# Output projection and shared expert: transposes inside the group before, products two blocks ahead across the turn, first inputs fetched during attention

## The reference

```python
xn  = layernorm(x)
x   = x + attention(xn) @ W_o          # 16 heads of 16, causal
        + routed(xn)                   # 16 experts of inner width 1024, each takes its 512 best tokens
        + gelu(xn @ Sg.T) * (xn @ Su.T) @ Sd.T    # shared expert, inner width 512
```

## Time and profile before

| | us |
|---|---|
| median of three runs | 2456.82 |
| the profiled execution, its own time | 2440.34 |
| its span | 2438.2 |
| TensorE matmul busy | 2319.6 (95%) |
| VectorE busy | 1935.7 (79%) |
| ScalarE busy | 1502.7 (62%) |
| GpSimd busy | 241.9 (10%) |
| mean granted clock of TensorE | 0.967 |

### The profile page before, as it was taken

How to read it: one execution, slowest core, us unless ns; L and a number is a source line. 1 busy time by engine, 2 the same in 40 slices (tenths; PEclk the granted TensorE clock), 3 DMA queues, 4 the chain that set the end, 5 groups by cost and what they waited for, 6 DMA issues and landing times. The chain is left out here.

```text
span 2438.2 us, 53041 instructions
## 1 busy us (share of the span) xinstructions
PE 2319.6 (95%) x20269; PEld 1506.5 (62%) x20275; DVE 1935.7 (79%) x3721; ACT 1502.7 (62%) x2908; POOL 241.9 (10%) x228
## 2 busy tenths in 40 slices
PE   7987999999999999999999999987898999999997
PEld 4554555555555555555555555547787888888886
DVE  6775999999999898999999999946744666666664
ACT  2233677788877777888788887762233545454543
POOL 3000000000000000000001000001121223322332
PEclk9956999999999999999999999998899999999998
DMA  7854000003000005000001000002252444344534
GB/s 263 314 156 82 17 10 10 4 11 79 12 8 11 14 17 108 22 13 10 11 2 40 4 4 4 4 24 73 69 165 88 128 132 134 91 131 131 138 98 119
DMA packets 141910, 167.91 MB, mean 69 GB/s; under 512 B 53612, under 2 KB 107372, under 8 KB 141628
## 3 DMA queue, kind: packets, MB, share of 16 engines
q1 hardware_dynamic: 127916, 142.87, 19.2%
q0 software_dynamic: 13728, 22.28, 4.9%
q10 hardware_dynamic: 64, 0.02, 0.0%
HBM read 117.86 MB, written 48.56 MB: 68 GB/s over the span
## 5 line engine op out<-in xcount | busy, mean ns | idle before, releaser
L945 DVE TENSOR_REDUCE a_mp<-a_pm 128x1 f32<-128x512 f32 (+3 forms) x2176 | 1293.2, 663 | 81.5 <-PE a_pm L1112 55.7
L1070 ACT ACTIVATE a_p<-a_ps 128x512 f32<-128x512 f32 (+2 forms) x2176 | 1120.9, 587 | 372.6 <-PE a_ps L1193 265.8
L1112 PE MATMUL a_pm<-a_k,a_q 48*128 48x512 f32 (+3 forms) x2304 | 820.6, 447 | 7.8 <-ACT p_xs L379 1.2
L1193 PE MATMUL a_ps<-a_q,a_k 50*128 50x512 f32 (+3 forms) x2304 | 762.2, 428 | 24.4 <-DMA a_q<-a_nb 23.4
L1193 PEld LDWEIGHTS a_ps<-a_q,a_k 50*128 50x128 f32 x2304 | 378.4, 188 | 387.8 <-ACT a_p L1070 306.8
L1215 PE MATMUL a_po<-a_p,a_v 128*32 128x384 f32 (+2 forms) x8688 | 615.5, 386 | 0.9
L1112 PEld LDWEIGHTS a_pm<-a_k,a_q 48*128 48x128 f32 x2304 | 384.2, 190 | 53.7 <-DVE a_mp L945 39.4
L1215 PEld LDWEIGHTS a_po<-a_p,a_v 128*32 128x32 f32 x8688 | 202.7, 109 | 202.2 <-issue 134.4
L1590 ACT ACTIVATE e_g<-e_pg 128x512 f32<-128x512 f32 x128 | 76.6, 599 | 242.4 <-PE e_pu L1668 242.0
L1635 DVE TENSOR_TENSOR e_hf<-e_g,e_pu 128x512 f32<-128x512 f32 x128 | 88.0, 688 | 172.1 <-ACT e_g L1590 163.2
L1678 PE MATMUL e_po<-e_wdp,e_hp 128*128 128x256 f32 x1536 | 203.3, 284 | 0.0
(11 more groups left out here) (161 smaller groups left out, 1672.4 us busy)
## 6 DMA issues: line engine op xcount, KB each, us to landing
e_wgu<-in_wg SPq DMA_DIRECT2D x18, 1024.0 KB, 5.6
e_wgu<-in_wu SPq DMA_DIRECT2D x18, 1024.0 KB, 7.7
e_wd<-in_wd SPq DMA_DIRECT2D x18, 1024.0 KB, 10.0
a_q<-q_parts SPq DMA_DIRECT2D x180, 64.0 KB, 2.3
q_parts<-p_parts SPq DMA_DIRECT2D x16, 512.0 KB, 6.0
k_parts<-p_parts SPq DMA_DIRECT2D x16, 512.0 KB, 7.5
a_k<-k_parts SPq DMA_DIRECT2D x60, 128.0 KB, 3.6
v_padded<-p_v SPq DMA_DIRECT2D x8, 544.0 KB, 7.7
```

What stands on the lines that cost most here:

```text
L945: eng.tensor_reduce(mp[:, i, heads[0]:heads[-1] + 1, r, kc], ps[:, 0:len(heads) * w].rearrange("p (a n) -> p a n", n=w), AX.X, ALU.max).th ...
L1070: eng.activation(pr[:, i, heads[0]:heads[-1] + 1, off:GT], pS[n % HEADS][:, 0:len(heads) * w].rearrange("p (a n) -> p a n", n=w), ACT.Exp) ...
L1112: last = eng.matmul(ps[:, n * w:(n + 1) * w], QT[t % SLOTS][tile, a, r * P:(r + 1) * P], KT[g % 2][tile, a, kc * GT:kc * GT + w], start=n ...
L1193: last = eng.matmul(ps[:, m * w:(m + 1) * w], KT[TILES[t][0] % 2][tile, a, b * P:(b + 1) * P], QT[t % SLOTS][tile, a, off:GT], start=m == ...
```

## The change

1. The groups of tokens are taken in reverse: group g of the program is now the tokens of group 7 - g.
2. Three inputs are fetched during attention, behind the end of tile 27 of 0 to 31: tokens and attention rows of the first group and attention rows of the second. They lie in room that the queries (`a_qr`) and keys (`a_k`) of finished tiles have left. GpSimd makes the halves of the first group's tokens there too, at the end of its attention program.
3. TensorE's order in a group is projection, up 2, down 0, *turn 0 of the next group*, up 3, down 1, *turn 1 of the next*, *up 0 of the next*, down 2, down 3, *up 1 of the next*. `m_at` has two buffers. The very first second half is turned into `m_po`.
4. VectorE's order: block 1, block 2, low half 0 of the next group, block 3, low half 1 of the next, block 0 of the next, additions. ScalarE follows the same order.
5. GpSimd converts the tokens of group g once the four products of group g - 2 are through, instead of once its down products are. Each kind of input has a semaphore and a place in SP's queue of its own.
6. The loops over groups are written out.

The core of the diff (lines of before have -, of the changed kernel +):

```diff
+                    if w == OVER[LAST - 4] + 5:
+                        eng.wait_ge(s_pv, START[LAST - 3])
+                        for n in range(2):
+                            eng.wait_ge(s_as[n], 16 * 13)
+                        eng.dma_start(k.XT0.rearrange("p d n -> p (d n)"), k.xt[NG - 1]).then_inc(k.s_xt0, 16)
+                        for n, room in enumerate((k.A0, k.A1)):
+                            eng.dma_start(room, k.attn.rearrange("(g k p) d -> g p k d", k=TG, p=P)[NG - 1 - n]
+                                          ).then_inc(k.s_a0, 16)
...
+                eng.wait_ge(k.s_xt0, 16)
+                eng.tensor_copy(k.XP0[:, :, HIGH, :], k.XT0).then_inc(k.s_xp0, 1)
+                eng.wait_ge(k.s_xp0, 1)
+                low(eng, (k.XP0[:, :, HIGH, :], k.XP0[:, :, LOW, :]), k.XT0).then_inc(k.s_xp0, 1)
...
+        def turned_in(g, d):
+            return pO[1] if (g, d) == (0, 1) else pT
...
-                for s in range(2):
-                    fetch(s, s)
-                    eng.sem_inc(s_out[s], 16)
...
+                tokens(1)
+                for g in range(2):
+                    inputs(g)
                 for g in range(NG):
+                    if g + 2 < NG:
+                        if g > 0:
+                            eng.wait_ge(s_xl, g)
+                        tokens(g + 2)
+                        eng.wait_ge(s_t, DC * (g + 1))
+                        attended(g + 2)
...
-                for g in range(NG):
-                    i, s = g // 2, g % 2
-                    eng.wait_ge(s_dn, IC * g + IC)
-                    eng.wait_ge(s_xin[s], 16 * i + 16)
+                for g in range(1, NG):
+                    s = g % 2
+                    if g > 1:
+                        eng.wait_ge(s_gu, IC * (g - 1))
+                    eng.wait_ge(s_xin[s], 16 * (g // 2) + 16 * s)
                     eng.tensor_copy(XP[s][:, :, HIGH, :], XT[s][:, :, :]).then_inc(s_xh, 1)
...
+                for d in range(DC):
+                    attended(0, d)
+                hidden(0, 0)
+                for g in range(NG):
+                    if g == LISTED:
+                        lists.close_dve(eng, pI)
+                    hidden(g, 1)
+                    hidden(g, 2)
+                    if g + 1 < NG:
+                        attended(g + 1, 0)
+                    if g == LISTED:
+                        lists.turn_dve(eng, pI)
+                    hidden(g, 3)
+                    if g + 1 < NG:
+                        attended(g + 1, 1)
+                        hidden(g + 1, 0)
+                    added(g)
...
-                    for d in range(DC):
-                        eng.wait_ge(s_al, DC * g + d + 1)
-                        for t in range(TG):
-                            last = eng.transpose(pT[:, t * P:(t + 1) * P], A[s][:, t, d * P:(d + 1) * P],
-                                                 k.identf[:, :])
-                        last.then_inc(s_t, 1)
-                        if d == 0:
-                            eng.wait_ge(s_xl, g + 1)
-                        up(g, s, d)
-                    eng.wait_ge(s_al, DC * (g + 1) + 1)
+                    eng.wait_ge(s_al, DC * (g + 1))
                     eng.wait_ge(s_oe, TG * g + TG)
...
+                    up(g, 2)
+                    down(g, 0)
+                    if g + 1 < NG:
+                        turn(g + 1, 0)
+                    up(g, 3)
+                    down(g, 1)
+                    if g + 1 < NG:
+                        turn(g + 1, 1)
+                        up(g + 1, 0)
+                    down(g, 2)
+                    down(g, 3)
+                    if g + 1 < NG:
+                        up(g + 1, 1)
...
+            k.QR = k.sb("a_qr", [P, 8 * GT], F32R)
+            k.XP0 = k.QR[:, 0:4 * GT].rearrange("p (d s n) -> p d s n", d=DC, s=2)
+            k.XT0 = k.QR[:, 4 * GT:6 * GT].bitcast(F32).rearrange("p (d n) -> p d n", d=DC)
+            k.A0 = k.QR[:, 6 * GT:8 * GT].bitcast(F32).rearrange("p (t d) -> p t d", t=TG)
+            k.A1 = k.ROOM[:, off:off + TG * D].bitcast(F32).rearrange("p (t d) -> p t d", t=TG)
```

186 lines of the change are left out of this document (98 added, 88 removed).

## The result

| | us |
|---|---|
| changed kernel, median of four runs | 2423.76 (2419.76 to 2425.82) |
| kernel before, beside it, median of four | 2456.26 (2451.05 to 2457.03) |
| ratio | 0.9885, 95% interval 0.9847 to 0.9924 |
| profiled execution of the changed kernel | 2422.2, span 2420.5 |

A forecast was written before the change was run, and what follows sets the result against it. TensorE was taken as busiest (95% of the span), standing still mainly before the output projection for VectorE's low half. Gains 14.0 + 12.1 + 1.7 - 1.5 = 26.3 us, off the runs' median, gave 2430.5 us; range 2422 to 2443.

The forecast's parts named there:

- Start of the stage: From the stage's first turn to projection 1: inputs already in place, projection 1 at 1677.1 instead of 1691.08, gain 14.0 us.
- Groups 1 to 3: Projections 1 to 4, the groups with list work: three periods of 24.9 us, 74.7 instead of 86.79, gain 12.1 us.
- c: Time GpSimd's token conversion takes from VectorE in a listed group: 1.2 us, with 0 and 2.9 as ends.
- TensorE's wait 2.4 us: Wait before the projection in groups 1 to 3, for the previous group's additions; 2.4 us, too short to lower the clock.
- Rival (b): Groups 1 to 3: the clock falls at a wait of 2.4 us too; period 26.6, 2437.3 us, chance 0.17.
- rival (a): GpSimd takes 2.9 us from VectorE in every listed group, clock falls in each; period 28.3, 2444.1 us, chance 0.19.
- Groups 4 to 7: Groups without list work, bound by TensorE: one wait of 1.11 us and three of 0.2 go, gain 1.7 us.
- Attention: GpSimd's first conversion beside VectorE's threshold bits, for which TensorE waits: loss of 1.5 us, bounded by 0 and 3.5.
- The note in the prediction: Base of the forecast: the runs' median lay 16.5 us above the profiled 2440.34 us; the gain was taken off the median.

The follow-up runs named there:

- late halves: Changed kernel, with GpSimd making the first halves of the tokens only near the end of attention; median 2421.9 us, ratio to before 0.9887.
- nothing early: Changed kernel, with the three early transfers and the halves moved from attention to the start of the stage; median 2431.1 us, ratio to before 0.9920.
- even steps: Changed kernel, with five of the 15 threshold steps of tile 28 made two to four tiles earlier; median 2409.9 us, ratio to before 0.9869.
- additions first: Changed kernel, with VectorE's additions ahead of the next group's first block; median 2420.7 us, ratio to before 0.9878.
- conversion later: Changed kernel, with GpSimd's conversion released by the last down product of the group before instead of its last products; median 2438.4 us, ratio to before 0.9963.

## Why the prediction was right, and where it was not

- **Start of the stage, 14.0 us forecast, 14.4 measured.** First turn, the first products at the low clock, VectorE's chain from the first product on, as worked out. The early fetch alone is worth 6.5 of it, as the experiment without it shows (7.5 where the clock came back sooner).
- **Groups 1 to 3, 12.1 forecast, 13.65 measured.** The new wait for the additions is there, and the period without a fall of the clock is 24.53 (24.9 forecast; the terms of the prediction add up to 23.61 + c, not 23.7 + c, so 24.8 would have been right). Two sizes were off and cancel in part. Group 4's first block, which stands in the third period, has no lists: 2.7 us less on VectorE, and the period becomes TensorE's own 22.56. I had multiplied by three without looking at which group a block belongs to. Against that the clock fell in the second, 1.5 us.
- **"TensorE's wait 2.4 us. That is under the 2.93 behind which the clock fell, so I leave the clock up":** the wait was shorter, 1.84 us, and the clock fell behind it in four of ten cases (one of two in the first trace, both in the second, none in late halves and in nothing early, one in even steps). The waits that I had seen bring the clock down, 2.93 and 5.84 us, said nothing of what a shorter one does. Rival (b), with 1.7 us for each of the three periods, came true in part: in this trace once, at 1.5 us. (Its sum, like that of rival (a), leaves out the 1.7 us of the last groups without a reason.)
- **How large is c:** 1.34 us against 1.2; moved by one semaphore it was 3.0, with another order 1.0. That the kinds of instructions under the conversion set it, and not its length, is now shown by experiment: it is the same conversion each time. The section of the Trainium skill's page "SBUF — State Buffer" that the prediction weighed, "Who interferes with whom", fits these rows: the caught steps at 1.72, 2.03, 1.26 and 2.87 us all have two inputs in SBUF, the product from PSUM at 0.68 has one. The list step of 1.06 us with a single input in SBUF (additions first) is not covered by it as the prediction put it; whether it ran in one of the two-port modes which the section excepts, no run shows.
- **Groups 4 to 7, 1.7 forecast, 3.6 measured** from projection 4 to the experts' first transposes. The waits went as said; besides that a group takes 20.48 us instead of 21.1 (projection to projection in the groups 5 to 7, the latter in both traces of the kernel before), of which the vanished wait is only 0.2. What the other 0.45 us of each are wasn't tried.
- **Attention, 1.5 us forecast.** The direct part is right: one step of 1.72 instead of 0.16 us. The step of the prediction that failed is the one that made this the whole price. The profile showed VectorE working without a pause and TensorE waiting for the counts; I took the wait as a sum of microseconds and did not ask what a stretch with such waits does to the clock, although I had just costed that for the projection. Measured: in both traces of the changed kernel a stretch of 34 and 55 us at 1.2 GHz, by which attention took 17.7 and 22.7 us longer, and 15 of its 16 executions in the upper group. What that costs the kernel beyond what it paid before is less, since the kernel before was in its own upper group in half of its executions.
- **Why the total came out near all the same:** I subtracted from a median of 2456.82, which lay in the upper group of the kernel before, so a fall in tile 28 was in that base already. 2456.8 - 31.6 (stage) + 1.6 (direct) = 2426.8, and the 16 executions have a median of 2425.8. Against the lower group (2440.8) the gain would have been 15 us. That the total came out near is in this part luck: all three executions behind the 2456.82 were of the upper group, which holds half of all. The note in the prediction, that the profiled execution lay 16.5 us under the median, was the sign of the two groups; I carried the difference over without asking what it was.

## What to carry to other kernels

A dense burst of small steps on a second engine, for which TensorE waits a few tenths of a microsecond each, cost far more here than the waits: look for such a place in the granted clock, over many executions, and try to spread it. Before work is put beside such a place, ask which of its instructions it will hold up, not how long it lasts. And where a profile's time lies far from the median of the runs, find out why before a difference is carried from the one to the other.

## What the runs showed of the hardware that I had not expected

- The clock fell to 0.50 behind waits of 0.70 and 0.34 us (late halves, 1576) in a place with five waits of 0.2 to 0.7 us within 21 us, and stayed up behind the same waits in the traces of the kernel before and of nothing early. What decides it from one execution to the next is open.
- Seven traces have a long stretch there: 0.50 for 31 to 58 us, with TensorE counted busy nearly throughout, up to within 2 us of the end of the tile. Two of them (additions first, conversion later) have a shorter one ahead of it, from which the clock was back after some 7 us. At the projections it was back at 1.00 after 4 to 8 us. What tells the long stretches from the short ones is open.
- A list step with one bfloat16 input in SBUF took 1.06 instead of 0.28 us beside GpSimd's cast, and GpSimd's cast itself took 1.81 instead of 1.04 us there (both in group 1 of additions first): each can be held up by the other.
